# Second cross-attention's key folds in two 64-row halves, 16 causal maxima ahead of the steps instead of 20, and the last normalisation split over steps

## What is computed

```python
x = x + _L0_xattn_ref(_layernorm(x), ctx, ...)     # 8 heads, 32-wide queries and keys
x = x + _L0_ffn_ref(_layernorm(x), ...)            # causal attention, 16 heads of 8; then a mixture of 4 experts
x = x + _L1_xattn_ref(_layernorm(x), ctx, ...)     # 16 heads of 64
x = x + _L1_ffn_ref(_layernorm(x), ...)            # 64 small networks of 16 units

# _L1_xattn_ref
k, v = split(ctx @ Wkv); q = x @ Wq                # heads of 64
dots = q k^T * 64 ** -0.5, masked by query rows; out = (softmax(dots) v) @ Wout + bout

# _L0_ffn_ref
h = conv(norm(x)); q, k, v = split(h @ attn_w); rotate q and k
p = softmax(causal(q k^T / sqrt(8))); x = x + (p v) @ proj_w
h = norm(x); e = argmax(h @ router_w)              # one expert per row
x = x + (silu(h @ wg[e]) * (h @ wu[e])) @ proj[e]
```

## Time and profile before

| what | us |
|---|---|
| three runs | 343.56 median (342.61 to 343.8) |
| profiled execution | 344.2, its span 342.4 |
| TensorE busy | 317.1 (93%), 2270 matmuls |
| TensorE weight loads | 221.3 (65%) |
| VectorE busy | 248.9 (73%) |
| ScalarE busy | 216.5 (63%) |
| POOL busy | 127.7 (37%) |
| chain that ended last | PE 57%, DVE 17%, ACT 13%, issue 5%, POOL 4%, DMA 3% |
| mean granted clock | 0.989 |

### The profile page before, as it was taken

One profiled execution on the slowest core, in us unless ns is written; L12 is line 12 of the kernel. 1 busy time (PEld: TensorE's weight loads), 2 busy tenths in 40 slices (PEclk: granted clock), 3 DMA queues, 4 the chain that ended last, 5 costly groups with the idle time before them and its releaser, 6 DMA issues.

```text
span 342.4 us, 6803 instructions
## 1 busy us (share of the span) xinstructions
PE 317.1 (93%) x2270; PEld 221.3 (65%) x2270; DVE 248.9 (73%) x766; ACT 216.5 (63%) x641; POOL 127.7 (37%) x183
## 2 busy tenths in 40 slices
PE   8799989998989999997999998998999899999886
PEld 2348778664544333354544998995678687878675
DVE  4988875884889999988352563379787867888476
ACT  1488885374466755564378664764776576676995
POOL 3455563110732444403231360410685525545400
PEclk9999999999999999998799999999999999999999
DMA  7590000086752520090002003100100000000002
GB/s 210 192 278 5 2 0 2 9 264 173 208 190 72 138 74 3 11 351 15 2 17 71 2 23 101 50 0 0 56 17 17 1 2 0 3 0 0 2 0 64
DMA packets 21881, 22.47 MB, mean 66 GB/s; under 512 B 3894, under 2 KB 18646, under 8 KB 21846
## 3 DMA queue, kind: packets, MB, share of 16 engines
q1 hardware_dynamic: 18982, 16.78, 17.0%
q10 hardware_dynamic: 2352, 4.20, 3.8%
q0 software_dynamic: 512, 1.05, 1.0%
HBM read 14.22 MB, written 7.60 MB: 64 GB/s over the span
## 4 chain that ended last, share of the span: by engine, by line
PE 57%; DVE 17%; ACT 13%; issue 5%; POOL 4%; DMA 3%; SPq 0%; ACTq 0%; POOLq 0%
PE PS L1388 51%; PE PS L1442 5%; DVE PS L873 5%; ACT big L1176 5%; ACT big L1364 3%; POOL big L529 2%; DVE big L691 2%; DMA big<-in_A_WkT 2%; DVE big L716 2%; ACT big L1306 1%; DMA XN<-scr_y,pos 1%; ACT big L1150 1%; DVE XN L668 1%; POOL big L531 1%; DVE mraw L705 1%
## 5 line engine op out<-in xcount | busy, mean ns | idle before, releaser
L1388 PE MATMUL PS<-big 128*128 128x128 f32 (+10 forms) x592 | 94.6, 311 | 9.1 <-DVE mB L873 4.1
L1388 PEld LDWEIGHTS PS<-big 128*128 128x128 f32 (+3 forms) x592 | 56.4, 151 | 42.9 <-DVE mB L873 21.3
L529 POOL TENSOR_TENSOR big<-big,urec 128x1024 f32<-128x1024 f32 x24 | 45.6, 1898 | 60.2 <-DVE urec L723 45.5
L1176 ACT ACTIVATE big<-big 128x154 f32<-128x154 f32 x192 | 60.5, 318 | 10.9 <-DVE big L691 5.6
L873 DVE CUSTOM_DVE_ANT_0 PS<-PS,later 128x128 f32<-128x128 f32 (+3 forms) x128 | 59.9, 516 | 8.8 <-PE PS L1388 7.6
L1306 ACT ACTIVATE big<-PS 128x1024 f32<-128x1024 f32 (+3 forms) x64 | 42.8, 701 | 31.1 <-PE PS L1388 31.1
L1150 ACT ACTIVATE big<-PS 128x1280 f32<-128x1280 f32 (+2 forms) x30 | 32.3, 1087 | 27.0 <-PE PS L1442 24.5
L1388 PE MATMUL PS<-kkC,XT 128*128 128x462 f32 (+1 forms) x96 | 36.0, 511 | 2.2 <-DVE big L716 2.2
L517 POOL TENSOR_TENSOR rstd<-ve,minus_half 128x4 f32<-128x4 f32 (+2 forms) x13 | 13.2, 1016 | 61.8 <-DVE ve L663 61.8
L1176 ACT ACTIVATION_READ_ACCUMULATOR big<-big 128x1 f32 x192 | 36.1, 188 | 0.0
L1388 PEld LDWEIGHTS PS<-vwCm,big 128*128 128x128 f32 x256 | 30.9, 192 | 3.9 <-ACT big L1150 1.3
(11 more groups left out here) (193 smaller groups left out, 507.0 us busy)
## 6 DMA issues: line engine op xcount, KB each, us to landing
scr_qk<-big SPq DMA_DIRECT2D x12, 384.0 KB, 3.3
big<-scr_qk SPq DMA_DIRECT2D x16, 288.0 KB
big<-in_wv ACTq DMA_DIRECT2D x1, 2048.0 KB, 8.0
scr_x<-zrow SPq DMA_DIRECT2D x2, 448.0 KB, 6.4
scr_y<-big SPq DMA_DIRECT2D x2, 448.0 KB, 3.5
X<-in_x ACTq DMA_DIRECT2D x2, 256.0 KB, 3.4
big<-in_A_WoT ACTq DMA_DIRECT2D x1, 512.0 KB, 4.7
cw<-in_C_Wk SPq DMA_DIRECT2D x1, 512.0 KB, 5.3
```

The costliest lines, as they stand in the source:

```text
L529: pool.tensor_tensor(pn[:, 0:GH * P].rearrange("p (h k) -> p h k", h=GH), Pt[u % 3][:, :, 0:KM], r.to_broadcast([P, GH, KM]), ALU.mult).th ...
L1176: i = act.activation(Pt[u % 3][:, h, :], Pt[u % 3][:, h, :], ACT.Exp, accum_out=usum[:, u % 3, h:h + 1])
L1388: return pe.matmul(o, lhsT, rhs, start=start, stop=stop)
```

## The change

Jobs of `PREC` go from 50 to 42. `kz` becomes `kT`, one unpadded copy of both heads' keys in one instruction; a chunk's two `kk` become one job with two matmuls on rows 0 to 63 and 64 to 127, in two banks, copied by one instruction where the banks are neighbours and by two where not (the last). `vT` holds seven chunks instead of four, so `vw` and `vr` come later in the list. The banks are handed out by `fold_banks`, from three rings: (0, 1, 2) for jobs 0 to 7, (0, 1, 2, 3) up to 27, (4, 7) from 28 on; `FOLD_AFTER` is the job whose copy has to be done first. Job 8 waits for sequence 0's rotation. 28 jobs stand ahead of the maxima, none of them behind `queries_keys(1)`; 14 stand after the scores 1 to 14. Scores 0 to 3 have waits of their own, and sequence 1's queries and keys go to banks 5, 6, 4, 7. `values(0)` and `no_values(0)` on ScalarE stand ahead of job 28's copy. 16 maxima go ahead, 48 in 24 steps. The turns of chunks 2 to 7 go from steps 3, 7, 11, 15, 20, 23 to 4, 8, 12, 16, 20, 24; rank, bias and weight copies go one step later. Sequence 0's norm `ln_m(0)` is cut: attention added in step 20, statistics in 21, aggregation and variance in 22, `x_plus_u(0)` in 24; `normalise_group(1, 0)` and `weigh_last` go to step 25. On POOL `ln_rsqrt` of that norm and `split_maxima(7)` go ahead of `apply_m(0)`.

```diff
-        F_UNIT = (3, 6, 9)
-        F_QKV = (14,30)
-        F_LN = 26
-        F_LATE = 32
-        F_VALUES = 42
-        F_MAX = 45
+        F_UNIT = (3, 6)
+        F_QKV = (10, 28)
+        F_WIDE = 8
+        F_LN = 23
+        F_LATE = 28
+        M_FOLDS = range(1, 15)
+        M_CHUNK0 = 10
+        F_MAX = F_LATE + M_CHUNK0
...
                 if c < HC // 2:
-                    yield "k", c, 2
-                    yield "v", c, 1
+                    yield "k", c
+                    yield "v", c
                 if c >= 1:
-                    yield "kk", 2 * c - 2, 1
-                    yield "kk", 2 * c - 1, 1
-                if c in (2, 4):
-                    for b in range(B):
-                        yield "vw", (c // 2 - 1, b), 1
-                        yield "vr", (c // 2 - 1, b), 1
-            for g in (2, 3):
+                    yield "kk", c - 1
+                if c in (5, 6):
+                    yield "vw", (0, c - 5)
+                    yield "vr", (0, c - 5)
+            for g in range(1, HC // 4):
                 for b in range(B):
-                    yield "vw", (g, b), 1
-                    yield "vr", (g, b), 1
+                    yield "vw", (g, b)
+                    yield "vr", (g, b)
...
-        def fold_bank(n):
-            if n < F_LATE:
-                return n % 3
-            return 7 if n % 2 else 4
         for b in range(B):
-            PREC.insert(F_QKV[b], ("xv", b, 1))
-        N_PREC = sum(j[2] for j in PREC)
+            PREC.insert(F_QKV[b], ("xv", b))
+        N_PREC = len(PREC)
+        assert len(M_FOLDS) == N_PREC - F_LATE
+        FOLD_BANKS, FOLD_AFTER = [], []
+        def fold_banks():
+            used, at = {}, 0
+            for n, (kind, _) in enumerate(PREC):
+                ring = (0, 1, 2) if n < F_WIDE else (0, 1, 2, 3) if n < F_LATE else (4, 7)
+                if n in (F_WIDE, F_LATE):
+                    at = 0
+                if kind == "kk" and at % len(ring) == len(ring) - 1:
+                    at += 1
+                banks = [ring[(at + j) % len(ring)] for j in range(2 if kind == "kk" else 1)]
+                at += len(banks)
+                FOLD_BANKS.append(banks)
+                FOLD_AFTER.append(max(used.get(k, 0) for k in banks))
+                for k in banks:
+                    used[k] = n + 1
+        fold_banks()
...
+        HALVES = (slice(0, 64), slice(64, P))
+        QKV_BANK = ((3, 4, 5, 6), (5, 6, 4, 7))
...
-        Z_OWN, Z_CTX, Z_EARLY, Z_WOUT, Z_SLOT, Z_ALL = 1, 2, 5, 6, 8, 15 + SLOTS
+        Z_OWN, Z_CTX, Z_EARLY, Z_WOUT, Z_SLOT, Z_ALL = 1, 2, 5, 6, 8, 14 + SLOTS
...
-        M0 = 20
-        M_STEPS = 22
+        M0 = 16
+        M_STEPS = 24
...
-        S_CHUNK = (None, 0, 3, 7, 11, 15, 20, 23)
-        S_SPLIT = {2: 2, 6: 3, 10: 4, 14: 5}
+        S_CHUNK = (None, 0, 4, 8, 12, 16, 20, 24)
+        S_SPLIT = {3: 2, 7: 3, 11: 4, 15: 5}
...
-        S_CB = 26
-        S_RANK = 24
-        S_COPY = 27
+        S_CB = 27
+        S_RANK = 25
+        S_COPY = 28
...
-            pool.memset(kz, 0.0).then_inc(zeroed, 1)
...
+            ln_rsqrt("m", (0,))
+            split_maxima(7)
...
             for b in range(B):
-                ln_rsqrt("m", (b,))
+                if b:
+                    ln_rsqrt("m", (b,))
...
-                if b == 0:
-                    split_maxima(7)
...
-            def ln_m(b):
-                ln_stats("m", U, b, lambda: dve.wait_ge(attn_added, b + 1))
-                x_plus_u(b)
+            def ln_m_first():
+                dve.wait_ge(attn_added, 1)
+                for n in range(QT):
+                    own(dve.bn_stats(stats[:, n, :], U[:, n, :]))
+            def ln_m_second():
+                own.wait()
+                for n in range(QT):
+                    own(dve.bn_aggr(mv[:, n, :], stats[:, n, :]))
+                own.wait()
+                dve.tensor_scalar(ve[:, 0:QT], mv[:, 0:QT, 1], EPS, None, ALU.add).then_inc(ln_var["m"], 1)
...
-                    ln_m(0)
+                elif s == S_TAIL + 3:
+                    ln_m_first()
+                elif s == S_TAIL + 4:
+                    ln_m_second()
...
+                elif s == M_STEPS:
+                    x_plus_u(0)
+                elif s == M_STEPS + 1:
...
-                elif s == S_RANK:
...
                 for n in range(n0, n1):
-                    kind, i, _ = PREC[n]
+                    kind, i = PREC[n]
...
-                    bank = fold_bank(n)
+                    bank, last = FOLD_BANKS[n][0], FOLD_BANKS[n][-1]
                     if kind == "k":
-                        if n == 0:
-                            act.wait_ge(zeroed, Z_ALL)
-                        for j in range(2):
-                            r = slice(64 * j, 64 * j + 64)
-                            copy(kz[r, i % 2, j, :], PS[r, bank, 0:B * KEYS], float(HDC) ** -0.5).then_inc(preC_act, 1)
+                        copy(kT[:, i % 2, :], PS[:, bank, 0:B * KEYS], float(HDC) ** -0.5).then_inc(preC_act, 1)
                     elif kind == "v":
-                        copy(vT[:, i % 4, :], PS[:, bank, 0:B * KPAD]).then_inc(preC_act, 1)
+                        copy(vT[:, i % VC, :], PS[:, bank, 0:B * KPAD]).then_inc(preC_act, 1)
                     elif kind == "kk":
-                        copy(kkC[:, :, i * KEYS:(i + 1) * KEYS],
-                             PS[:, bank, 0:B * KEYS].rearrange("p (b k) -> p b k", b=B)).then_inc(preC_act, 1)
+                        o = kkC[:, :, 2 * i * KEYS:(2 * i + 2) * KEYS].rearrange("p b (j k) -> p j b k", j=2)
+                        if last == bank + 1:
+                            q = copy(o, PS[:, bank:last + 1, 0:B * KEYS].rearrange("p j (b k) -> p j b k", b=B))
+                        else:
+                            for j in range(2):
+                                q = copy(o[:, j], PS[:, FOLD_BANKS[n][j], 0:B * KEYS].rearrange("p (b k) -> p b k", b=B))
+                        q.then_inc(preC_act, 1)
...
-            copy_C(F_LN, F_VALUES)
-            act.wait_ge(preC_act, sum(j[2] for j in PREC[:F_VALUES]))
+            copy_C(F_LN, F_LATE)
+            act.wait_ge(preC_act, F_LATE)
...
-            copy_C(F_VALUES, F_MAX)
+            copy_C(F_LATE, F_MAX)
...
-            copy_C(F_MAX, len(PREC))
+            copy_C(F_MAX, N_PREC)
...
-                done = [0]
-                for kind, i, k in PREC:
-                    done.append(done[-1] + k)
                 for n in range(n0, n1):
-                    kind, i, _ = PREC[n]
-                    bank = fold_bank(n)
+                    kind, i = PREC[n]
+                    banks = FOLD_BANKS[n]
+                    bank = banks[0]
...
-                    if n == F_LATE:
+                    elif n == F_WIDE:
+                        pe.wait_ge(qkv_read, 4)
+                    elif n == F_LATE:
...
-                    elif 3 <= n < F_LATE:
-                        pe.wait_ge(preC_act, done[n - 2])
-                    elif n >= F_LATE + 2:
-                        pe.wait_ge(preC_act, done[n - 1])
-                    if n == F_MAX:
+                    if n >= F_MAX and LN_BANK in banks:
...
+                    after = FOLD_AFTER[n]
                     if kind == "kk":
-                        pe.wait_ge(preC_act, done[1 + PREC.index(("k", i // 2, 2))])
+                        after = max(after, 1 + PREC.index(("k", i)))
                     elif kind in ("vw", "vr"):
-                        pe.wait_ge(preC_act, done[1 + PREC.index(("v", 2 * i[0] + 1, 1))])
+                        after = max(after, 1 + PREC.index(("v", 2 * i[0] + 1)))
+                    if after:
+                        pe.wait_ge(preC_act, after)
...
                     elif kind == "kk":
-                        q = mm(PS[:, bank, 0:B * KEYS], wqT[:, i // 2, :], kz[:, (i // 2) % 2, i % 2, :])
+                        for j, half in enumerate(HALVES):
+                            q = mm(PS[:, banks[j], 0:B * KEYS], wqT[half, i, :], kT[half, i % 2, :])
...
                         for c in range(2):
-                            q = mm(PS[:, bank, 256 * c:256 * c + 256], vT[:, (2 * g + c) % 4, b * KPAD:b * KPAD + KM],
+                            q = mm(PS[:, bank, 256 * c:256 * c + 256], vT[:, (2 * g + c) % VC, b * KPAD:b * KPAD + KM],
...
-                            q = mm(PS[32 * j:32 * j + 32, bank, 0:D], vT[:, c % 4, b * KPAD + KM:b * KPAD + KPAD],
+                            q = mm(PS[32 * j:32 * j + 32, bank, 0:D], vT[:, c % VC, b * KPAD + KM:b * KPAD + KPAD],
...
-                if m >= 3:
+                if m == 2:
+                    pe.wait_ge(s_max, 1)
+                elif m == 3:
+                    pe.wait_ge(qkv_read, 4 * B)
+                elif m >= 4:
...
-                if m >= 2 and late < len(PREC):
+                if m in M_FOLDS:
...
-                if late == F_MAX:
+                if m == M_CHUNK0:
...
```

(23 more changed lines are left out.)

## The result

The changed kernel takes 350.27 us (median of 14 runs, 344.45 to 353.93), the kernel before beside it 343.68 (14 runs, 341.99 to 351.94). The ratio is 1.0067, 95% interval 1.0036 to 1.0098. Forecast was 340.6, faster; it is slower and outside the range of 337.8 to 344.9. The 14 times fall in two groups with a mean granted clock of their own: 344.5 to 347.6 at 0.975 to 0.990 (7 runs, median 345.28) and 352.9 to 353.9 at 0.955 to 0.961 (7 runs). The ratio compares the lower group of either kernel; how often the upper one comes is part of the result.

A forecast was written before the change was run, and what follows sets the result against it. No engine bounds the whole: TensorE is busiest but alternates with VectorE in the causal steps. Terms -3.5 + 0.3 - 2.4 + 2.6 = -3.0 give 341.2 profiled, 340.6 us as median; range 337.8 to 344.9.

The forecast's parts named there:

- The sum of -3.0: Whole kernel: -3.5 + 0.3 - 2.4 + 2.6 = -3.0 us on the profiled execution of 344.2, so 341.2.
- rival A: Wait for the slots: it also costs the clock, seven us at 1.2 GHz, 2.5 us; total 343.1; chance 0.22.
- wait for split 7: Steps 20 to 24: 1.5 us of the split norm's gain is lost waiting for POOL's split of chunk 7's maxima.
- Front: Folds and sixteen maxima ahead of the steps: step 4 starts 3.5 us sooner, bounds 1.5 and 4.6.
- the folds' stalls: Sixteen maxima ahead: late folds delay scores that VectorE wants, 2.4 us in all; maxima end at 104.0.
- rival B: Step 0 gains nothing from fewer maxima, as sequence 1's stores and loads land late: gain 1.5, total 342.6; chance 0.10.
- Turns one step later: Steps 4 to 20: each chunk's split falls in its turn's step, costing 0.3 us for chunks 2 to 6, bounds 0 and 5.
- rival C: Turns of maxima come too early, TensorE waits about 1 us for each of chunks 2 to 6: 345.6; chance 0.12.
- Steps 20 to 25: Split norm's stretch: 14.6 us instead of 17.06, VectorE setting it; gain 2.4 us, bounds 1 and 4.
- Placement one step later: Rank and placing of rows one step later: slots and their gate come late, costing 2.6 us, bounds 1.5 and 3.5.
- Rival D: Placing is hidden after all, since steps 25 to 31 take ScalarE longer with moved weight copies: 338.8; chance 0.11.
- the 0.12 us above one fold: Key folds of second cross-attention: a pair of 64-row halves takes 0.53 + 0.12 = 0.65 us; eight chunks save 3.3 us.

The follow-up runs named there:

- the later series: Four series of runs of the kernel before, taken beside the follow-up kernels; medians 343.80, 343.67, 344.80 and 345.32 us.
- the kernel with all three waits filled: Changed kernel plus unread matrix products of ones in TensorE's waits ahead of step 0, chunk 7's turn and the slots' turn: 340.68 us, ratio 0.9925.
- The run with the stores first: Changed kernel with chunk 0's stores of maxima issued on SyncE ahead of the third part's transfers of sequence 1: 345.91 us, ratio 1.0065.
- the first wait filled: Changed kernel plus six unread matrix products of ones in TensorE's wait ahead of step 0: 343.04 us, ratio 0.9985.
- the kernel with 20 and 22 steps, spread and filled: Changed kernel with 20 maxima ahead, 44 in 22 steps, late folds over 19 maxima, five unread products in step 0's wait: 338.41 us, ratio 0.9793.
- DVE's half alone: Kernel before with only DVE's part of the split norm, GpSimd's order kept as before: 346.70 us, ratio 1.0042.
- the split norm alone: Kernel before with only sequence 0's norm split, on DVE and GpSimd: 339.81 us, ratio 0.9886; measured again 341.21 us, ratio 0.9871.
- the one with 30 folds ahead as well: Changed kernel with chunk 0's stores ahead of the third part's transfers and 30 folds ahead of the maxima instead of 28: 346.45 us, ratio 1.0072.

## Why the prediction was wrong

**The step that failed is the clock.** The sum of -3.0 has no term for it, and rival A has one fall of 2.5 us, at the slots. The trace shows three falls: 20 us behind 1.53 us of waiting ahead of step 0, 3 us at the turn of chunk 7, 7 us at the slots. The first costs 8 us where it happens, by the two groups of times (352.9 to 353.9 against 344.5 to 347.6), and filling the other two waits gives 2.4. The kernel before has runs 8 us up as well, 2 of 14 here and 6 of 80 in the later series, and no trace shows one of them; the changed kernel has 7 of 14, and even its lower group is 4.6 us over the kernel with all three waits filled (345.28, 340.68). I compared gaps by length alone: 2.15 costs the clock, 0.62 busy of 2.00 us does not the earlier trace rows. The 1.5 us wait for split 7, which I did foresee, I put down as idle time and left its clock at 1.00 (the text says "clock 1.00 through step 25"). And ahead of step 0 I had no wait.

**Front** (forecast: step 4 sooner by 3.5 us). With the clock held step 0 is 1.55 sooner and step 20 2.43. Two terms were mis-sized. The first maximum was to come at 87.3; with the changed kernel it comes at 88.71, with the waits filled at 88.03, hardly before 88.41. The folds ahead take longer than summed: a pair 0.72 to 0.76 instead of 0.65, and two full folds between pairs 1.25 instead of 1.06, so that the turn of sequence 1 comes at 79.31 (waits filled) instead of 78.6. And the first eight maxima were to be undisturbed to 95.8, but end near 97.5, with the waits filled: GpSimd's split starts behind them at 97.48 (98.16 in the changed kernel's execution, 95.76 before). I set the folds' stalls at 2.4 us in sum but did not see that most fall in the first eight, for which part three, stores and step 0 wait. That is rival B's place and my own bound of 1.5. The run with the stores first adds that the stores weren't the only thing that ended there: DVE's sixteenth maximum ended with them.

**Turns one step later** (0.3): step 0 to step 20 takes 47.75 us with the clock held, and took 48.63, so there is no loss; rival C is refuted.

**Steps 20 to 25** (14.6 instead of 17.06): 153.23 to 167.79 is 14.56. Right, with the wait for split 7, and at a kept clock only.

**Placement one step later** (+2.6): from step 25 to the slots it is 14.00 us before and 15.24 with the first wait filled, so 1.2 more, and the wait is 1.49 (2.75 in the profiled execution of the changed kernel), where I said 1.8. The 1.8 and 0.5 of idle time that I named make 2.3; the last 0.3 of my 2.6 stands in no row. Rival D is refuted. Together with the clock behind it this is rival A, which so came true, but as the smaller part.

**Bounds.** With all three waits filled the change gives 340.68, and I had said 340.6. This agreement is partly luck: up to step 20 the change gained 0.8 us less than forecast, and the placement cost 1.4 less. The halves give 1.4 us in the kernel with filled waits, the split norm 4.0 by itself, part of it clock; together this is more than the whole change gives with its clock held (343.8 to 340.7, by 3.1). That points to 16 maxima ahead with 24 steps as the part that costs, but doesn't show it: the kernel with 20 and 22 steps, spread and filled, has a ratio of 0.9793 against 0.9925. These two differ also in how the late folds are spread and in the fillings, so the share of each stays open.

**The halves.** I took the 0.12 us above one fold as all that the alternation costs. The Trainium skill, TensorEngine Tiling (Array Packing), Key Properties, says that a change of tiling mode drains TensorE. The traces agree: two full folds take 1.25 us between pairs of halves and 1.06 where no halves stand beside them. The same page's speedup of up to 2x for halves (Theoretical Speedup) isn't reached: 0.72 to 0.76 a pair, where one full fold takes 0.53.

## What to carry to other kernels

Give every wait of TensorE that a change makes or moves a price for the clock behind it, also when it is only 1.2 to 1.5 us long (one fall here stands behind 0.60): one stall taken away came back here as three, and the clock cost more than all the work that was saved. Where a wait can't be removed, spread the work that TensorE has left over it, or fill it, and see whether the spread of the times goes. And when a unit's work is cut in pieces, follow the other engine's queue as well: DVE's half alone made the kernel slower (1.0042), both halves took 4.0 us off.

## What the hardware showed

- After a wait of 1.20 to 1.53 us TensorE's clock falls in some executions and not in others, and can then stay at 0.50, the 1.2 GHz level, for 20 us (109 to 129 us in the changed kernel) although TensorE is busy 2.00 of 2.00 us in the windows shown. Windows behind a wait of 1.29 us each, first the kernel with the stores first (wait ends at 106.11, run 345.64), then the one with 30 folds ahead as well (105.22, run 351.94):

```profile
108.00:110.00 2.00, 2.00 (x14) 0.57 (x14) 2.00 (x8) 1.66 (x3) 0.99 (x3) 1.00 0.75 219
108.00:110.00 2.00, 2.00 (x12) 0.35 (x9) 1.81 (x6) 1.49 (x3) 0.83 (x2) 0.50 0.60 170
```

- Shorter waits don't exclude it. With the split norm alone the clock is 0.50 at 112 to 114 us (for some 3 us in all), and the last wait before is 0.60 us long and ends at 108.18; the kernel before and the one with DVE's part alone keep 1.00 there behind 0.61.
- Longer waits don't bring it for certain. The profiled changed kernel keeps its clock after a wait of 1.55 us that ends at 248.54, while it loses it after 1.53 us ahead of step 0:

```profile
112.00:114.00 2.00, 2.00 (x14) 0.74 (x7) 0.68 (x3) 0.07 (x1) 0.27 (x1) 0.50 0.04 6
247.00:249.00 2.00, 0.46 (x1) 0.30 (x2) 1.93 (x5) 1.66 (x11) 0.00 (x0) 1.00 0.00 0
```

- At waits of 2.69 and 2.15 us it fell in the profiled executions too, for 10 and 7 us. What decides whether it falls and for how long, I can't say from these runs.
- 64-row float32 halves of 308 columns in different banks overlap, but not fully: 0.72 to 0.76 us a pair, against 0.53 for one 128-row fold and 1.04 to 1.06 for two. Two full folds between such pairs take 1.25 us instead of 1.06.
